# Output in two half-row arrays: two scatter-adds per expert, no second sum, row numbers copied by VectorE

## What is computed

```python
topk_w, topk_idx = jax.lax.top_k(scores, K)        # 8 of 64 experts per token
dest = jnp.where(valid, slot_expert * CAP + pos, E * CAP)   # CAP = 128 slots each
xb = buf[:E * CAP].reshape(E, CAP, h)
gate = jnp.einsum('ech,ehf->ecf', xb, w_gate)
up = jnp.einsum('ech,ehf->ecf', xb, w_up)
hmid = jax.nn.silu(gate) * up
yb = jnp.einsum('ecf,efh->ech', hmid, w_down).reshape(E * CAP, h)
slot_out = yb[dest] * topk_w.reshape(-1)[:, None].astype(yb.dtype)
out = jnp.zeros((T, h), yb.dtype).at[slot_token].add(slot_out)
x = x + out
```

## Time and profile before

| | us |
|---|---|
| median of 3 runs | 1436.13 |
| runs, lowest to highest | 1434.30 to 1439.93 |
| profiled execution, its own time | 1430.09 |
| its span, first to last instruction | 1428.3 |
| first gather of the expert stage issued | 1068.37 |
| last scatter-add issued | 1394.93 |
| final sum issued | 1400.02 |

### The profile page before, as it was taken

One profiled execution on the slowest core, in us unless ns is written; L12 is line 12 of the kernel. 1 busy time (PEld: TensorE's weight loads), 2 busy tenths in 40 slices (PEclk: granted clock), 3 DMA queues, 4 the chain that ended last, 5 costly groups with the idle time before them and its releaser, 6 DMA issues. The chain is left out here.

```text
span 1428.3 us, 19290 instructions
## 1 busy us (share of the span) xinstructions
PE 1220.8 (85%) x6510; PEld 891.9 (62%) x6510; DVE 742.1 (52%) x1427; ACT 504.6 (35%) x1145; POOL 503.5 (35%) x533
## 2 busy tenths in 40 slices
PE   0788999887999987799998779999349999999990
PEld 0567777655777765577776557777145666666660
DVE  6674645576576658568666847443641222222220
ACT  1681322565322167422216643121222233323320
POOL 2520333633033373303346330221005455555541
PEclk9999999998999999899999999999658999999995
DMA  7002221000242100033200002641417999999957
GB/s 263 1 1 91 81 108 54 0 1 31 91 141 81 54 1 1 31 115 116 107 28 1 1 31 114 233 153 42 199 68 247 338 338 353 355 348 359 276 85 132
DMA packets 45600, 181.07 MB, mean 127 GB/s; under 512 B 6412, under 2 KB 9484, under 8 KB 36692
## 3 DMA queue, kind: packets, MB, share of 16 engines
q1 hardware_dynamic: 30660, 140.23, 26.2%
q0 software_dynamic: 14864, 39.85, 12.2%
HBM read 149.36 MB, written 34.90 MB: 129 GB/s over the span
## 5 line engine op out<-in xcount | busy, mean ns | idle before, releaser
L2001 PE MATMUL PS<-WE,XGT 128*128 128x384 f32 x512 | 195.2, 505 | 1.5 <-DVE HM L1577 0.8
L656 POOL CAST HH<-HID 128x512 fp32r<-128x512 f32 x44 | 34.0, 773 | 343.2 <-DVE HID L1483 343.2
L786 ACT ACTIVATE P<-PS,NM 128x512 f32<-128x512 f32 (+3 forms) x256 | 132.0, 534 | 50.4 <-DVE NM L1194 49.2
L1600 PE MATMUL PS<-XTH,WHI 128*128 128x512 f32 x352 | 142.9, 406 | 1.0 <-ACT SIL L929 1.0
L1436 DVE TENSOR_TENSOR WLO<-WRAW,WHI 128x584 fp32r<-128x584 f32 (+1 forms) x88 | 109.7, 1247 | 62.8 <-ACT WHI L915 57.0
L1601 PE MATMUL PS<-XTL,WHI 128*128 128x512 f32 x352 | 140.3, 399 | 0.0
L1602 PE MATMUL PS<-XTH,WLO 128*128 128x512 f32 x352 | 140.3, 399 | 0.0
L915 ACT ACTIVATE WHI<-WRAW 128x1280 fp32r<-128x1280 f32 x44 | 56.2, 1277 | 207.0 <-DMA WRAW<-in_ffn 204.1
L2001 PEld LDWEIGHTS PS<-WE,XGT 128*128 128x128 f32 x512 | 88.2, 192 | 57.8 <-issue 23.5
L1194 DVE TENSOR_REDUCE NM<-PS 128x2 f32<-128x1024 f32 (+2 forms) x96 | 98.6, 1041 | 44.8 <-PE PS L1609 44.3
L1660 PE MATMUL PS<-ident,P 128*128 128x128 f32 x640 | 97.5, 289 | 22.8 <-ACT P L786 12.8
(11 more groups left out here) (269 smaller groups left out, 2748.0 us busy)
## 6 DMA issues: line engine op xcount, KB each, us to landing
WE<-in_we SPq DMA_DIRECT2D x64, 1152.0 KB
WRAW<-in_ffn SPq DMA_DIRECT2D x44, 932.0 KB, 4.6
acc<-HN SPq DMA_DIRECT2D x17, 256.0 KB, 4.6
XIN<-in_x SPq DMA_DIRECT2D x4, 1024.0 KB, 9.2
out<-X SPq DMA_DIRECT2D x4, 1024.0 KB, 4.2
out<-acc POOLq DMA_DIRECT2D x1, 4096.0 KB, 23.3
hx<-HN SPq DMA_DIRECT2D x3, 1152.0 KB, 8.7
CTX<-in_ctx SPq DMA_DIRECT2D x4, 256.0 KB, 6.7
```

The lines of the kernel that those rows point to most:

```text
L786: act.activation(prob(t, n), PS[:, c0:c0 + (t + 1) * P], ACT.Exp, bias=NM[:, c:c + 1], accum_out=SSUM[:, c:c + 1]).then_inc(S["p_ready"], 1)
L1600: pe.matmul(dst, a[0], b_[0], start=first, stop=False, **kw)
L2001: mm = pe.matmul(bank(2 + s % 2, 0, 2 * F1), XGT[s % 2][:, k, :], WE[s][:, k * 2 * F1:(k + 1) * 2 * F1], start=(k == 0), stop=(k == KC - 1))
```

## The change

- The output becomes two arrays, `out_left` and `out_right`, of 256 columns each (`CH`). `acc`, its zeroing and the final sum go. The host joins the two halves, which is a copy.
- Every expert has two scatter-adds, one of the left and one of the right half of `YE`, each of 128 rows. Each waits for the one before into its own array, which now is that of expert e - 1.
- `added` is raised ahead of the right half, behind the wait for `y_sb`.
- VectorE copies the row numbers into `IDX1`: the first 12 in one go as soon as `IDX` is there, then from expert 4 on one per expert, that of expert e + 8, behind its `HM`. Since the tile was that of expert e - 4, VectorE waits until both halves of that one have landed. GpSimd only waits for the copy.
- The stores of x into the output become two, and waits on `out_stored` count accordingly. VectorE's first 4 experts stand ahead of its loop.

```diff
-                sp.dma_start(rows(out[span(b, T), :], NT), X[:, :, :]).then_inc(S["out_stored"], 16)
+                for h in range(2):
+                    sp.dma_start(rows(out[h][span(b, T), :], NT), X[:, :, h * CH:(h + 1) * CH]).then_inc(
+                        S["out_stored"], 16)
...
             def gather(e, s):
 
-                alone(pool, "pool")
-                pool.tensor_copy(IDX1[s][:, :], IDX[:, bass.ds(e, 1)]).then_inc(M["idx"], 1)
                 pool.wait_ge(M["idx"], 1 + e + 1)
...
             def scatter(e, s, r):
 
-                if not isinstance(r, int) or r > 0 or s > 1:
-                    pool.wait_ge(scattered[s % 2], 16 * (r * (NX // 2) + s // 2))
-                    alone(pool, "pool")
-                pool.sem_inc(M["added"], 1)
                 pool.wait_ge(M["y_sb"], 1 + e + 1)
-                alone(pool, "pool")
-                pool.indirect_dma_start(out=(out, acc)[s % 2],
-                                        out_offset=bass.IndirectOffsetOnAxis(ap=IDX1[s][:, 0:1], axis=0),
-                                        in_=YE[s % NY][:, :], in_offset=None, compute_op=ALU.add,
-                                        ).then_inc(scattered[s % 2], 16)
+                for h in range(2):
+                    if not isinstance(r, int) or r > 0 or s > 0:
+                        pool.wait_ge(scattered[h], 16 * (r * NX + s))
+                        alone(pool, "pool")
+                    if h == 1:
+                        pool.sem_inc(M["added"], 1)
+                    half = slice(h * CH, (h + 1) * CH)
+                    pool.indirect_dma_start(out=out[h],
+                                            out_offset=bass.IndirectOffsetOnAxis(ap=IDX1[s][:, 0:1], axis=0),
+                                            in_=YE[s % NY][:, half], in_offset=None, compute_op=ALU.add,
+                                            ).then_inc(scattered[h], 16)
...
-            for parity in range(2):
-                pool.wait_ge(scattered[parity], 16 * (E1 // 2))
-            pool.dma_start(out[0:NTOK, :].rearrange("(a f) c -> a (f c)", f=NT),
-                           acc[0:NTOK, :].rearrange("(a f) c -> a (f c)", f=NT),
-                           accum_op=ALU.add, max_dma_last_dim=8192).then_inc(combined, 16)
-            pool.wait_ge(combined, 16)
+            for h in range(2):
+                pool.wait_ge(scattered[h], 16 * E1)
...
+            def rows_of(e, s):
+
+                dve.tensor_copy(IDX1[s][:, :], IDX[:, bass.ds(e, 1)]).then_inc(M["idx"], 1)
+
+            def rows_ahead(e, s):
+
+                for h in range(2):
+                    dve.wait_ge(scattered[h], 16 * (e + AHEAD - NX + 1))
+                rows_of(e + AHEAD, (s + AHEAD) % NX)
+
+            dve.wait_ge(idx_ready, 1)
+            for e in range(NX):
+                rows_of(e, e)
...
                 gated(e, s, r)
-            experts(dve, expert, 1, E1)
+                if not isinstance(e, int) or NX - AHEAD <= e < E1 - AHEAD:
+                    rows_ahead(e, s)
```

More of the change, by code:

```diff
@@ L84, in end, with build @@
         assert self.n == self.per, (self.sem, self.n, self.per)
-def build(nc, x, ctx_in, w, out, hx, acc):
+def build(nc, x, ctx_in, w, out, hx):
     place = {"at": 16896}
@@ L321, in build @@
     M = {n: sem("m_" + n) for n in ("idx xgt_ps xgt_sb gu_ps sil wc hm_twice hm hmt_ps hmt_sb y_ps y_sb added".split())}
-    scattered = [sem("scattered_even"), sem("scattered_odd")]
-    acc_zeroed, combined = sem("acc_zeroed"), sem("combined")
+    scattered = [sem("scattered_left"), sem("scattered_right")]
     lists_loaded, spread_loaded, idx_ready = sem("lists_loaded"), sem("spread_loaded"), sem("idx_ready")
@@ L479, in _ @@
             sp.dma_start(hx[NTOK:ROWS, :], ZR[:, :]).then_inc(S["hx_stored"], 16)
[L480 to L484, removed]
+            for h in range(2):
+                sp.dma_start(out[h][NTOK:ROWS, :], ZR[:, 0:CH]).then_inc(S["out_stored"], 16)
             for dst, src in LISTS:
@@ L749, in _ @@
                 gather(e, e)
-            pool.wait_ge(S["out_stored"], 16 * (B + 1))
-            pool.wait_ge(acc_zeroed, 16 * (ROWS // P))
+            pool.wait_ge(S["out_stored"], 32 * (B + 1))
             for e in range(NX - AHEAD):
@@ L1420, in x1 @@
                     dve.tensor_tensor(X[:, t, :], bank(2 + t), XIN[:, t, :], ALU.add).then_inc(S["x1_ready"], 1)
-                dve.wait_ge(S["out_stored"], 16 * (a + 1))
+                dve.wait_ge(S["out_stored"], 32 * (a + 1))
                 stats(row_x, x1, "x1_ready", NT * a)
@@ L1592, in expert @@
                 gated(e, s, r)
-            experts(dve, expert, 1, E1)
+                if not isinstance(e, int) or NX - AHEAD <= e < E1 - AHEAD:
+                    rows_ahead(e, s)
+            for e in range(1, 5):
+                expert(e, e, 0)
+            experts(dve, expert, 5, E1)
             expert_T(E1 - 1, 1)
@@ L2122 @@
           for k, v in arrays.items()}
-    out = nc.dram_tensor("out", (ROWS, C), F32, kind="ExternalOutput").ap()
+    out = [nc.dram_tensor(n, (ROWS, CH), F32, kind="ExternalOutput").ap() for n in ("out_left", "out_right")]
     hx = nc.dram_tensor("hx", (ROWS, HROW), F32, kind="Internal").ap()
-    acc = nc.dram_tensor("acc", (ROWS, C), F32, kind="Internal").ap()
-    build(nc, ap["x"], ap["ctx"], ap, out, hx, acc)
+    build(nc, ap["x"], ap["ctx"], ap, out, hx)
     r = run(nc, [arrays], core_ids=[0])
-    return r.results[0]["out"][0:NTOK].reshape(B, T, C)
+    return np.concatenate([r.results[0][n][0:NTOK] for n in ("out_left", "out_right")], 1).reshape(B, T, C)
```

## The result

The changed kernel takes 1550.82 us (median of 4 runs, 1543.3 to 1555.24); the kernel before, run beside it and earlier, 1435.22 us (4 runs). The ratio is 1.0789, with a 95% interval of 1.0757 to 1.0821. The forecast was 1476, range 1424 to 1535: slower, as forecast, but by 115.6 us and not by 40. The profiled execution is the fastest of the four, 1543.3 us with a span of 1541.5 (before: 1430.09 and 1428.3).

The account below looks back on a forecast made before the run. TensorE was taken to bound the expert stage before, landings of half scatter-adds one expert back after. -22.0 (end) - 0.3 (start) + 62.3 (steps) = +40.0 us: 1470 for the profiled execution, 1476 for the median, range 1424 to 1535.

Parts of the forecast that it names:

- The end: After the last scatter-add: final sum goes (23.9 us), right half issued 1.89 us later, closing 4.98 us stay; sum -22.0 us.
- the floor of 5.09: GpSimd's own work per expert in the expert stage: gather, left and right scatter-add, 1.31 + 1.89 + 1.89 = 5.09 us.
- VectorE's copy: Row-number copy in the expert stage: 0.14 us, fits where VectorE idles 2.60 us between HM and the next HMT copy.
- At the start: GpSimd's first row-number copy and wait (1.12 us) replaced by VectorE's copy: bounds -0.9 and 0, taken -0.3 us.
- the dropped zeroing and the split stores: 17 stores of zeros and SP's 4.1 us wait go, output store in two halves: edits counted at nothing.
- Between 5.09 and 7.5 I take 6.0 for the 52 steps under load: Landing wait per expert while weights load: 52 x 6.0 + 11 x 5.3 = 370.3 us, +62.3 over 307.95.
- the prediction's upper bound of 7.5: Landing wait per step under load: half of the excess of 9.89 over 5.09 us makes 7.5 us.
- A step is the largest of three: Per expert, the largest of TensorE's 4.93 us, GpSimd's own 5.09 us and the landing, between 5.09 and 7.5 us.
- GpSimd alone as the bound: Expert stage: landings short enough, steps of 5.09 to 5.35 us, 1427 to 1443 us; chance 0.16.
- TensorE as the bound: Expert stage: a half costs GpSimd about a gather and lands in time, steps stay 4.93 us, 1414 us; chance 0.12.
- Rival 3: Scatter queue under load: packets, not bytes, are waited for; 16 instead of 8 per engine, step near 7.5, 1560 us; chance 0.17.
- The clock: TensorE busy 82% at steps of 6.0 us; fall of its granted clock to 1.2 GHz given no chance of its own.

Follow-up runs that it names:

- four-array run: Changed kernel with its halves going by turns into four arrays, each waiting for the landing two experts back, extra arrays not summed: 1423.95 us, 0.9903 of before.
- run without reloads: Changed kernel without SP's weight loads from expert 12 on, those experts using the first twelve's weights: 1418.67 us, 0.9889 of before.
- one chain of halves: Changed kernel with the left scatter-add alone, right half of the experts' sums left out: 1485.65 us, 1.0355 of before.

## Why the prediction was wrong

**What held.** The bound before and the mechanism after: steps set by the one-back landing while weights fly; VectorE stopped behind its wait once GpSimd is late, and TensorE behind HMT; everything back to back once the weights are in. The four-array run and the run without reloads show it from both sides. The end came to -21.4 for -22.0, partly by luck: the last right half was issued 3.36 us after the left and not 1.89, since it had to wait for the landing of the right half before it, and the span ended 8.6 us after it and not 9.5. A half costs GpSimd 1.55 to 1.57 us, as taken (the whole 1.59), so the floor of 5.09 measured 5.06. VectorE's copy cost nothing measurable in the kernel before (1.0011). At the start, the way from the start of the VectorE instruction that writes `IDX` to the first gather went from 1.62 to 1.47 us, -0.15 where -0.3 stood; the -0.5 of the list above is another stretch, which the prediction did not have. That the dropped zeroing and the split stores cost or gain nothing no run shows by itself.

**What failed** is the step "Between 5.09 and 7.5 I take 6.0 for the 52 steps under load". In the terms of its sum, the first 52 steps took 381.0 us (7.33 each) where 312 stood, and the last 11 took 52.2 (4.75 each) where 58.3 stood: 125.3 us for 62.3. Over the first 48, those with weights on the way, a step was 7.43. That is close to the prediction's upper bound of 7.5, but by luck: the bound was worked out for one chain, and one chain of halves measured 6.37. Three reasons; the runs show the first two, the third is argued:

1. *Two chains, one step.* I worked out the wait of one chain and let the second half stand beside it. An expert is through only when both halves have got their turn, and a late right half puts off the next left one, as the timeline above shows. The flights of the first 48 experts average 6.1 us, but the longer one of each expert's two averages 6.9. One chain measures 6.37: the 6.0 was nearly right for that. This, with the next reason, is 1.06 of the missing 1.43.
2. *The second half lengthens the first one's flight.* I let the waiting behind the weights shrink with their share of the DMA engines, and the share did fall, to 44.9% (48.6 was reckoned). For one chain the flight shrank with it: whole rows average 5.76 us where they have 8.01 in the kernel before without its sum. But with both halves of an expert on the way a left half averages 6.12 us, and alone 5.44, though alone it has more weights beside it (54.2% of the engines). Without load a half flies 3.8 us either way. This is some 0.7 of the 1.06, and the later of two about the rest. (The kernels also differ in GpSimd's 1.85 us for the right half, and so in when things are issued.) Bytes did little: half of them gave about 0.30 us. In the changed kernel the median flight was 5.7:

```profile
q1 hardware_dynamic: 1955, 16.07, 44.9%
q0 software_dynamic: 5136, 7.79, 41.3%
...
out_right<-YE,IDX POOLq DMA_INDIRECT x14, 5.7
...
out_left<-YE,IDX POOLq DMA_INDIRECT x14, 5.7
```

(DMA queues of the changed kernel, 1200 to 1300 us: packets, MB, share; issues: count, median us to landing.) The same of the kernel with left halves alone:

```profile
q1 hardware_dynamic: 2374, 19.48, 54.2%
...
out_left<-YE,IDX POOLq DMA_INDIRECT x16, 4.9
```

3. *No way to catch up.* A step is the largest of three, and its floor of 5.06 lies above TensorE's 4.93. A prompt landing therefore never repays a late one, and the average of the maxima is above the maximum of the averages. I took the largest of three means. Only 2 of the 48 steps were at the floor (5.15 or less), and the longest took 10.12. With GpSimd's floor raised to 5.83 the step rose with it, to 7.80.

**The rivals.** GpSimd alone as the bound (5.09 to 5.35) is what the kernel becomes without load or with four arrays, 1418.67 and 1423.95: the state was real, the condition for it was not met. TensorE as the bound did not come, since a half costs GpSimd as much as a whole. Rival 3 comes nearest in time (1560) with its 7.5, but not by its mechanism as it was put: with the same 16 scatter packets per DMA engine the four-array kernel keeps 5.22. What it had right: shorter weight packets shortened the step, halving the bytes did little, and the left half's flight grew by 0.7 us when the right half's packets were there too. Whether those packets themselves or the other order of issues make the 0.7 stays open.

The rule of the Trainium skill's page "DMA: Bandwidth & Descriptors" ("Anatomy of one DMA — SWDGE (gpsimd) path"), by estimate 2.3 us for a half, stays below every flight measured, 3.6 us at the least. The same page of the Trainium skill, "SWDGE vs HWDGE vs iDMA", has each DMA engine serve its queues in turn; the 0.80 us that smaller weight packets bring agree with it, though no run shows the turns themselves.

**The clock.** I gave its fall no chance, since another stage kept 1.00 while TensorE was busy 78% of the time. Here the same 78% (178.60 of 230) came with 0.90, and the four matmuls after a stand of 3.70 us took 2.07 us, where four of the same shape took 1.03 before, at the granted clock of 1.00: the lower level, 1.2 GHz. The share alone does not tell; here the idle time came in pieces of up to 5.8 us. It was a small term at most. TensorE still waited for VectorE 65 us of the 300 from 1100 to 1400, and its rows are only some 8%, 29 us, of the chain that ended last between 1100 and 1450 us. Had all of these run at the lower level, half of them would be its price, an estimate of 15 us at the most. No run changes the clock alone. The row of before:

```profile
1246.57 1.03 PE L2017 MATMUL PS<-WE,HMT 128*128 128x256 f32 x4
```

**What stays open:** why a loaded flight reaches 9.6 us, beyond the part that goes with the weight packets' size and the part that goes with the other half; and whether spreading the last sum over the stage would have won the 22 us without the chain. No run here both computes everything and is faster than the kernel before. By estimate the four arrays with a sum of 22.1 us at the end come to 1446 (1423.95 and 22.1).

## What to carry over

A second accumulator is not only a sum to be paid at the end; it doubles the time a scatter-add has to land. Before one is taken out, price distance against the flight *under load, at its slow end*, times the number of steps: here 63 waits cost 125 us to save 22. Where several chains must all be through in a step and the floor leaves no slack, reckon with the later of their flights at its spread, not with a mean. And a large idle time on one engine's row (VectorE's 251.9 us) is to be tested by giving that engine its freedom before it is called the cause.

## What the hardware showed unexpectedly

- A scatter-add of 128 rows holds GpSimd for 1.55 to 1.60 us in most cases (1.64 at the longest) whether rows have 1024 or 2048 bytes; the bare flight is 3.7 to 4.0 against 4.7 to 5.0 us.
- Under the weight loads the flight of a half spreads from 3.6 to 9.6 us, of a whole row (kernel before without its sum) from 4.7 to 9.9 with a median of 7.6, and in the kernel before, at a DMA share of 1.04, TensorE is busy 230.00 of 230 us all the same, since two experts' time is given.
- With one chain of scatter-adds into one array a step is the mean flight and 0.91 to 0.93 us, loaded or not, with 1024 or 2048 bytes a row.
- Cutting the weight loads from packets of 9216 to 2304 B raised the stage's throughput from 237 to 267 GB/s and the DMA share from 0.85 to 0.98, because the experts passed faster (6.63 us a step for 7.43); their bytes are the same. Small packets might have been thought a loss.
